# Expert loops of TensorE and ScalarE written out tile by tile, in place of engine loops of four tiles

## What is computed

```python
logits = tokens.astype(jnp.float32) @ router_w.astype(jnp.float32).T
probs = jax.nn.softmax(logits, axis=-1)
rw, re = jax.lax.top_k(probs, TOP_K)              # TOP_K = 2
...
combine = jnp.zeros((N, E), tokens.dtype).at[jnp.arange(N)[:, None], re].set(rw)
out = tokens
for e in range(E):                                 # E = 8
    h = jax.nn.gelu(tokens @ w1[e] + b1[e], approximate=False)
    y = h @ w2[e] + b2[e]
    out = out + combine[:, e:e + 1] * y
```

## Time and profile before

| | us |
|---|---|
| median of 3 runs | 2516.29 (2516.2 to 2521.94) |
| the profiled execution | 2519.71 |
| its span, first to last instruction | 2518.0 |
| the expert ticks of the loop, 8 to 99 (copies to `xT` from 2151.4 to 2474.5) | 323.1 |

### The profile page before, as it was taken

How to read it: one execution, slowest core, us unless ns; L and a number is a source line. 1 busy time by engine, 2 the same in 40 slices (tenths; PEclk the granted TensorE clock), 3 DMA queues, 4 the chain that set the end, 5 groups by cost and what they waited for, 6 DMA issues and landing times. The chain is left out here.

```text
span 2518.0 us, 38803 instructions
## 1 busy us (share of the span) xinstructions
PE 2169.8 (86%) x11962; PEld 1810.5 (72%) x11963; DVE 1468.8 (58%) x2640; ACT 1141.0 (45%) x3408; POOL 1509.9 (60%) x1295
## 2 busy tenths in 40 slices
PE   5798689988998899889988998899999856887884
PEld 3486578877887788678877887788777755665553
DVE  7994577667766775677577757775333566000112
ACT  4420245555555455545554555455565310333332
POOL 1002677677767766777676767776666421555553
PEclk9998899999999899999999999999999757899997
DMA  7424622232222222222232222222333311555666
GB/s 236 164 63 156 215 72 83 83 90 70 84 85 88 71 81 82 88 74 82 81 90 73 81 82 84 80 82 81 90 88 88 110 52 44 174 177 171 193 197 211
DMA packets 156966, 270.51 MB, mean 107 GB/s; under 512 B 27733, under 2 KB 104548, under 8 KB 156808
## 3 DMA queue, kind: packets, MB, share of 16 engines
q0 software_dynamic: 59584, 161.78, 21.4%
q1 hardware_dynamic: 62220, 72.81, 9.2%
q10 hardware_dynamic: 35004, 33.93, 4.4%
HBM read 223.61 MB, written 45.77 MB: 107 GB/s over the span
## 5 line engine op out<-in xcount | busy, mean ns | idle before, releaser
L1124 POOL DMA_INDIRECT edge_G<-xn_scratch,edge_row_i x1029 | 1226.1, 1192 | 452.1 <-issue 279.2
L1185 ACT ACTIVATE edge_weighted<-edge_hots,bins_scale 128x128 f32<-128x128 bf16 x2401 | 738.4, 391 | 66.4 <-DVE edge_row_hots L1213 66.4
L1153 PE MATMUL edge_op<-edge_win,edge_A 128*128 128x256 f32 x2744 | 671.5, 388 | 43.9 <-issue 33.9
L1153 PEld LDWEIGHTS edge_op<-edge_win,edge_A 128*128 128x128 f32 x2744 | 526.5, 194 | 144.3 <-issue 55.1
L1149 PE MATMUL edge_op<-edge_G,edge_weighted 128*128 128x256 f32 x2058 | 517.0, 388 | 67.7 <-DMA edge_G<-xn_scratch,edge_row_i 48.3
L1176 ACT COPY edge_A<-edge_ap 128x512 f32<-128x512 f32 x343 | 201.1, 586 | 767.5 <-PE edge_ap L1140 632.8
L1208 DVE TENSOR_TENSOR edge_hots<-bins_iota128b,bins_recb 128x1024 bf16<-128x1024 bf16 x343 | 236.8, 690 | 419.9 <-PE edge_ap L1140 328.4
L1149 PEld LDWEIGHTS edge_op<-edge_G,edge_weighted 128*128 128x128 f32 x2058 | 370.9, 194 | 113.4 <-issue 51.8
L1140 PE MATMUL edge_ap<-edge_weighted,edge_row_hots 128*128 128x128 f32 x2744 | 370.4, 278 | 25.6 <-DMA edge_win<-xn_scratch 13.3
L1140 PEld LDWEIGHTS edge_ap<-edge_weighted,edge_row_hots 128*128 128x128 f32 x2744 | 341.4, 193 | 60.0 <-issue 19.2
L1213 DVE TENSOR_TENSOR edge_row_hots<-all_iota,bins_recd 128x512 f32<-128x512 f32 x343 | 235.0, 685 | 0.0
(11 more groups left out here) (286 smaller groups left out, 1906.5 us busy)
## 6 DMA issues: line engine op xcount, KB each, us to landing
exp_w1x<-in_w ACTq DMA_DIRECT2D x105, 256.0 KB
edge_G<-xn_scratch,edge_row_i POOLq DMA_INDIRECT x1029
exp_ys<-ys_scratch SPq DMA_DIRECT2D x12, 1024.0 KB
ln_xin<-in_x SPq DMA_DIRECT2D x12, 512.0 KB, 5.5
xn_scratch<-ln_xnb ACTq DMA_DIRECT2D x12, 512.0 KB, 5.9
xnT_scratch<-ln_xT SPq DMA_DIRECT2D x12, 512.0 KB, 7.0
mix_xg<-xn_scratch SPq DMA_DIRECT2D x12, 512.0 KB, 3.9
mix_ek<-xnT_scratch SPq DMA_DIRECT2D x12, 512.0 KB, 4.8
```

What stands on the lines that cost most here:

```text
L1124: pool.indirect_dma_start(out=G[:, row_buffer(b), i, :], out_offset=None, in_=xn_dram, in_offset=bass.IndirectOffsetOnAxis(ap=row_i[:, b * ...
L1153: last = nc.tensor.matmul(op[j][:, :], A[:, j, i, :], win[:, q % 2 * DN + i, :], start=False, stop=i == DN - 1)
L1185: last = nc.scalar.activation(weighted[:, buf, i, :], hots[:, b % 2, i // 2, :, i % 2], ACT.Copy, scale=scale[:, b, i:i + 1])
```

## The change

`ticks` loses its engine loop. All 107 ticks of TensorE and of ScalarE are written out, and every wait in them compares with a constant. GpSimd, SyncE and VectorE keep their code, and no transfer, product or copy is added, removed or resized.

```diff
-        def ticks(eng, count, tick):
-
-            for i in range(8):
-                tick(i, i // 4, i % 4)
-            with eng.Fori(2, NXT // 4 - 1) as four:
-                for j in range(4):
-                    tick(four * 4 + j, four, j)
-            for i in range(NXT // 4 * 4 - 4, count):
+        def ticks(count, tick):
+
+            for i in range(count):
                 tick(i, i // 4, i % 4)
...
-                ticks(pe, NXT + 2, tick)
+                ticks(NXT + 2, tick)
...
-                ticks(act, NXT + 2, tick)
+                ticks(NXT + 2, tick)
```

## The result

The changed kernel took 2501.39 us in the median of 20 runs (2491.46 to 2511.03), against 2518.49 us of the kernel before in 20 runs on the same chip (2506.27 to 2527.36). The ratio is 0.9933, with a 95% interval of 0.9919 to 0.9947. So it is faster by 17 us, where 67 us were forecast, and the time lies above the range of 2425 to 2488. The profiled execution took 2492.52 us.

What follows compares the result with a forecast made beforehand. No engine was full; handing work around bounds the expert loop's 3.51 us tick. At 2.74 us a tick 71 us go, less 4 for weights: 67 us, 2516.3 - 67 = 2449 us, range 2425 to 2488.

Steps and rivals of the forecast that it cites:

- What takes some of it back: Part of the forecast on losses in the 92 loop ticks: period 2.74 us, so 71 us go, less 4 us for late loads.
- the stops: Expert ticks: gelu waits 3.41 and 4.12 us for a product shown as finished; cause unnamed, period taken as 2.74 us.
- stops grow with the pace: Rival, expert loop: each 11.6 us loses about 3.4; period 3.15 to 3.69 us, times about 2475 to 2508; chance 0.11.
- The floor: GpSimd in the expert loop: 2.61 us from scatter to scatter is the shortest period, so at most 83 us can go.
- the 63.3 us of "issue": Before gelu in the loop: time in which ScalarE was said to wait for nothing but its own sequencer.
- TensorE as the bound: Rival: GpSimd is no floor, TensorE sets 2.39 to 2.43 us a tick; 101 us go, 2415 us; chance 0.05.
- Weights: Expert loop: loads issued three ticks ahead come late beside SP's 1 MB loads; 4 us lost, 12 at worst.
- Steps of the register waits: Loop's 642 ScalarE and 729 TensorE steps: 11 and 37 us by busy time, but priced by the ring's period instead.
- The instruction stream: Written-out ticks need about 14 instruction packets on TensorE and about as many on ScalarE, which could stop the ring.
- the rival "slower": Instruction packets stop the ring; over 3.0 us each turns the sign, 4 us each gives 2544 us; chance 0.06.
- The page weighed: Skill page's instruction-fetch rule: the loop's branch target stayed inside the held pages, so the gain would be nothing, against 71 us.
- What would show it: Marks in the loop: gelu's wait below 50 us, PEclk above 0.96, at most three waits over 3 us.

Runs made afterwards that it cites:

- the 2391 us level: Faster of two machine levels, named by the kernel before's time; both kernels rerun unedited there: before 2390.59 us, changed 2358.76 us, ratio 0.9845.
- constants: Changed kernel with ScalarE's expert number a constant, its lookup left out: 0.9857 where before takes 2391 us; 2469.5 us beside 2510.5 in single runs at the slower level.

## Why the prediction was wrong, step by step

- **The step that failed** is "What takes some of it back": the stops. From nine written-out periods with one stop among them I took 2.74 us, "the only mean in which stops are weighted by how often the trace has them". Measured was 3.33 us, a stop of 3.2 us in every third tile. Nine periods were too few, and six of them were the head, where the ring fills. The two rows that spoke of it were on the page: two stops, 11.6 us apart by their ends, both where tiles are short. The rival built on them, "stops grow with the pace", gave 3.15 to 3.69 us and 2475 to 2508 us; measured were 3.33 us and 2501 us. It had a chance of 0.11 and came near in its period (9.9 us for 11.6) and in its size (3.2 us for 3.4). That the total fits is luck in part: its own formula, with 9.9 and 3.2 in it, makes 3.86 us of the floor of 2.61, and 3.33 came out because between stops tiles take 2.1 to 2.4 us, below that floor, as the ring catches up out of its buffers. That it is a limit on pace is not shown.
- **What I read as cost of the loop was partly the level.** 3.51 - 2.74 = 0.77 us a tile was to go. At the level without stops the tile of before is 3.07 us, so 0.44 of it was never the loop's to give. There the forecast of the period holds: 2.76 us for 2.74, and the gain is 92 x (3.07 - 2.76) = 28 us; the medians differ by 32. A forecast from the profile at hand could not know the 3.07. But the 63.3 us of "issue" and the long steps were a warning. The text took "issue" for time in which ScalarE waited for nothing but its own sequencer; that can't be read from this trace, which lacks two in five of the updates. A wait on a product that stood finished, as in the earlier trace rows, is what a late release looks like.
- **The floor** was right: 2.61 us from scatter to scatter, unchanged lengths, and at the 2391 us level it is the largest part of the period (busy 73% of the stretch, as the text wanted; 61% at 2517 us, where stops hide it).
- **TensorE as the bound** under 2425 us: wrong, as thought. The run with one lookup less has its free tiles at TensorE's 2.38 and gains nothing in the mean.
- **Weights**: right, with room. TensorE's waits on `exp_w1x`, TensorE's two rows together, were 7.4 us in the stretch (3.0 for products, 4.4 for their weight loads), for the 12 that would have refuted it. Waits named "issue" in front of the same products are another 71 us by the same two rows; in the stop above they are for the copy to `xT`. In the complete trace at 2391 us it is 7.2 us for the weights.
- **Steps of the register waits**: right not to price them by their own length. At 2391 us 28 us went from the loop, more than ScalarE's 11, but only once both engines were rid of them.
- **The instruction stream**: the packets came nearly as counted, and no row shows that one stopped an engine. Before, the stretch had 6 and 1; after:

```profile
q8 instruction: 13, 0.21, 0.3%
q14 instruction: 18, 0.15, 0.2%
```

  12 more on each queue, for 14 estimated. At the 2391 us level, where the same code must be brought in as well, the stretch has the same 13 and 18 packets and the tiles are 2.76 us. What the packets cost was not measured apart. The sign of the rival "slower" never came near.
- **The page weighed** (the Trainium skill, Runtime: NRT & Kernel Launch, section Instruction fetch mechanics) would have had no gain, as the loop's body stayed resident; it calls the fetch one reason to unroll, not the only one. The runs have 17 us of gain, and 32 at the other level, so the measurement decides against using that rule alone for this loop.
- **What would show it**: gelu's wait on the first product fell to 58 us, not below 50 (as far as the records name it); the granted clock fell to 0.92 and did not rise above 0.96 (the other level shows the same fall without stops, so that mark was a poor one); five waits of over 3 us stood there on ScalarE and TensorE, for the three allowed. The text's own marks name the failed step.

**What stays open** is what brings the stops at the 2517 us level. They don't follow a count of ScalarE's instructions or a fixed time, and they stay without the 1 MB loads and without ScalarE's lookups. They shrink when the tiles between them are slower. What the trace shows of one is that TensorE's releases come late and together. A count of TensorE's instructions, a limit on how fast all engines together may go on, and the recording itself are three readings left. The run that would have told the first two apart, with instructions on an engine beside the path, never fell on that level; for the third it would take times without a recording. Open as well is what the looped form costs at 2391 us: that it is 0.31 us a tile when both engines lose it is measured, by which steps is not.

## What to carry to other kernels

Before a wait is priced as the code's, look whether the same wait stands in a stage of another structure: "remote" and "issue" in front of plain copies of the edge stage would have told that part of the idle time was not this loop's, and could still be there after the edit. Look also at whether the record is complete before "issue" is read as the sequencer's own time. A sample of a few periods gives the free pace of a ring and not how often it stops; where two short stretches each end in a stop, their distance deserves more than a chance of 0.11. And where two engines hand work to and fro, try both together: here each alone gave some 5 us of 37.

## What the runs showed that was not expected

- The same program at two levels: 2390 and 2501 to 2518 us for the kernel before, with 586 ns for the same copy at both, 86 us of the difference in the edge stage and 41 in the expert loop (323.1 against 282.4 us). A change has to be compared within one level; it was worth 0.9845 at one and 0.9933 at the other. The slower level is also the one whose traces lack two in five of the semaphore updates.
- The same edit moves the tile by other amounts at the two levels: writing out takes 0.18 us off it at 2517 us and 0.31 at 2391, nine increments on ScalarE add 0.03 and 0.29, constants take off 0.12 and 0.05.
- The granted clock of TensorE in the loop fell with the written-out form at both levels, from 0.96 to 0.92 and from 0.99 to 0.95. The stops of the one level don't explain it; where it was lost stays open.
- GpSimd keeps its 0.30 us of "issue" ahead of each transfer even when it is behind and TensorE waits for it.
